# Turning eleven instead of ten key tiles on VectorE, with the query projection one slot earlier, in the attention stage of a decoder layer

## The reference

```python
C_q = Q @ Wq_d                                   # 128 latent columns
C_kv = K @ Wkv_d                                 # 64 latent columns for each of 1601 keys
CqWqk = (C_q @ W_qk).reshape(b, n, 16, 64)       # one 64-column query for each head
scores = einsum('bnhl,bkl->bhnk', CqWqk, C_kv) / 8
attn = softmax(scores, axis=-1)
V_up = (C_kv @ Wv_u).reshape(b, nkv, 16, 64)
out = einsum('bhnk,bkhd->bnhd', attn, V_up)      # x = layernorm(x + out)
```

## Time and profile before

| | |
|---|---|
| median of three runs | 2862.83 us (2859.35 to 2862.97) |
| the profiled execution | 2854.49 us, span 2852.5 us |
| granted TensorE clock, mean | 0.977 |
| busy in the span: TensorE, VectorE, GpSimd, ScalarE | 92%, 79%, 68%, 59% |
| exchange, DMA issues | 1152 of 80 KB |

### The profile page before, as it was taken

How to read it: one execution, slowest core, us unless ns; L and a number is a source line. 1 busy time by engine, 2 the same in 40 slices (tenths; PEclk the granted TensorE clock), 3 DMA queues, 4 the chain that set the end, 5 groups by cost and what they waited for, 6 DMA issues and landing times. The chain is left out here.

```text
span 2852.5 us, 41197 instructions
## 1 busy us (share of the span) xinstructions
PE 2636.4 (92%) x14360; PEld 1988.6 (70%) x14360; DVE 2264.6 (79%) x2125; ACT 1671.3 (59%) x2611; POOL 1941.2 (68%) x1423
## 2 busy tenths in 40 slices
PE   6867889999999999999996999999999999999997
PEld 3645566666666666666664788888888888788885
DVE  1436568888887788878884799999999899899988
ACT  2242467777777777777775545444545555555553
POOL 1000247767777777767874888888887788888883
PEclk9979999999999999999998999999999999999999
DMA  7304566767777777677765132222222322232221
GB/s 263 120 31 171 170 227 201 222 194 207 216 216 213 226 215 220 199 235 243 226 200 186 55 108 96 74 74 74 74 67 91 109 75 89 74 116 77 74 96 74
DMA packets 166768, 420.60 MB, mean 147 GB/s; under 512 B 30113, under 2 KB 57634, under 8 KB 166050
## 3 DMA queue, kind: packets, MB, share of 16 engines
q1 hardware_dynamic: 161698, 407.93, 45.7%
q10 hardware_dynamic: 4864, 10.03, 0.9%
HBM read 248.43 MB, written 75.04 MB: 113 GB/s over the span
## 5 line engine op out<-in xcount | busy, mean ns | idle before, releaser
L1566 DVE SCALAR_TENSOR_TENSOR c_acc<-c_ps,c_sd,c_acc 128x1024 f32<-128x1024 f32 x448 | 573.2, 1282 | 97.0 <-PE c_ps L1422 96.9
L1160 POOL COPY b_pt<-b_tn 32x640 f32<-32x640 f32 x640 | 457.6, 715 | 262.6 <-DVE b_tn L1068 231.0
L1477 ACT ACTIVATE c_scaled<-c_ps,c_sgu 128x1024 f32<-128x1024 f32 x336 | 375.6, 1118 | 425.0 <-PE c_ps L1422 422.5
L1062 DVE TENSOR_REDUCE b_nm<-b_sc 128x1 f32<-128x1604 f32 x256 | 468.1, 1828 | 189.4 <-PE b_sc L899 188.2
L981 ACT ACTIVATE b_pr<-b_sc,b_nm 128x799 f32<-128x799 f32 (+1 forms) x512 | 476.9, 934 | 237.3 <-DVE b_nm L1062 214.7
L1649 POOL TENSOR_TENSOR c_sum_u<-c_sum_u,c_scaled 128x1024 f32<-128x1024 f32 x168 | 404.9, 2410 | 116.0 <-ACT c_scaled L1477 115.5
L1649 POOL TENSOR_TENSOR c_sum_g<-c_sum_g,c_scaled 128x1024 f32<-128x1024 f32 x168 | 405.0, 2411 | 82.5 <-ACT c_scaled L1477 82.4
L899 PE MATMUL b_sc<-b_kh,b_qs 128*128 128x402 f32 (+1 forms) x1024 | 403.3, 394 | 41.2 <-ACT b_pr L981 37.5
L918 PE MATMUL b_po<-b_pt,shared 128*64 128x256 f32 x2560 | 389.4, 392 | 29.5 <-DMA b_pt<-b_tn 29.1
L1068 DVE STREAM_TRANSPOSE b_tn<-b_pr 128x1280 f32<-128x1280 f32 x256 | 384.7, 1503 | 3.3 <-ACT b_pr L981 2.0
L899 PE MATMUL b_sc<-b_kl,b_qs 128*128 128x402 f32 (+1 forms) x1024 | 357.3, 349 | 0.0
(11 more groups left out here) (192 smaller groups left out, 4371.6 us busy)
## 6 DMA issues: line engine op xcount, KB each, us to landing
b_pt<-b_tn SPq DMA_DIRECT2D x1152, 80.0 KB, 2.7
c_uw_int<-wint_u SPq DMA_DIRECT2D x56, 512.0 KB, 3.4
c_gw_int<-wint_g SPq DMA_DIRECT2D x56, 512.0 KB, 3.4
c_dw_int<-wint_d SPq DMA_DIRECT2D x56, 512.0 KB, 3.4
a_cx<-in_b_ctxT SPq DMA_DIRECT2D x16, 1608.0 KB, 11.1
b_rw<-in_c_gw SPq DMA_DIRECT2D x28, 512.0 KB, 4.1
b_rz<-in_c_gz SPq DMA_DIRECT2D x28, 512.0 KB, 5.6
b_rw<-in_c_uw SPq DMA_DIRECT2D x28, 512.0 KB, 4.0
```

Source lines behind the costliest of these rows:

```text
L1062: V.tensor_reduce(nm[:, u % 2:u % 2 + 1], both, AXY, ALU.max, negate=True).then_inc(s_nm, 1)
L1160: G.tensor_copy(pt[s][32 * c:32 * c + 32, a, :, :], tn[s][32 * a:32 * a + 32, c, :, :]).then_inc(s_block, 1)
L1477: S.activation(dst[:, :], pair[SLOT[x, t] % 4][:, :], ACT.Identity, scale=scale(x, t)).then_inc(s_e, 1)
L1566: V.scalar_tensor_tensor(out=total, in0=pair[SLOT[x, t] % 4][:, :], scalar=scale(x, t), in1=total, op0=ALU.mult, op1=ALU.add).then_inc(s_a ...
```

## The change

NDT goes from 10 to 11, so VectorE turns 1408 columns instead of 1280, each block move has 704 columns instead of 640 (88 KB instead of 80 KB in each DMA), TensorE transposes two tiles instead of three, and the copy to `pe` has 256 columns instead of 384. `project` moves from k % 8 == 5 to k % 8 == 4 on all engines. The value product is cut into tiles 0 to 7 and 8 to 12. The key buffers `kh` and `kl` shrink from 1664 to 1608 columns, which makes room for the larger `tn` and `pt`.

```diff
-NDT = 10
+NDT = 11
...
+KSC = 1608
...
 def ring_events():
     out = [("project", 0, 0)]
     for k in range(NU + OUT_AT):
-        if k % 8 == 5 and k + 3 < NU:
-            out.append(("project", (k + 3) // 4, 0))
+        if k % 8 == 4 and k + 4 < NU:
+            out.append(("project", (k + 4) // 4, 0))
...
 def special(k):
-    return k in CN_AT or k % 8 == 5 and k + 3 < NU or k % 4 == OUT_AT % 4 and k >= OUT_AT
+    return k in CN_AT or k % 8 == 4 and k + 4 < NU or k % 4 == OUT_AT % 4 and k >= OUT_AT
...
-        kh = [sb(f"b_kh{j}", [P, KPAD], F32R) for j in range(2)]
-        kl = [sb(f"b_kl{j}", [P, KPAD], F32R) for j in range(2)]
+        kh = [sb(f"b_kh{j}", [P, KSC], F32R) for j in range(2)]
+        kl = [sb(f"b_kl{j}", [P, KSC], F32R) for j in range(2)]
...
-                for t in (range(0, 7), range(7, NKT))[part]:
+                for t in (range(0, 8), range(8, NKT))[part]:
...
             for k in range(NU + OUT_AT):
                 if k < NU:
                     scores(k, 1)
-                if k % 8 == 5 and k + 3 < NU:
-                    project((k + 3) // 4)
+                if k % 8 == 4 and k + 4 < NU:
+                    project((k + 4) // 4)
...
             for t in (kh[0], kl[0], kh[1], kl[1]):
-                ins = V.memset(t[:, NKV:KPAD].bitcast(F32), 0.0)
+                ins = V.memset(t[:, NKV:KSC].bitcast(F32), 0.0)
```

## The result

The changed kernel takes 2882.91 us (median of six runs, 2876.13 to 2888.77) against 2863.21 for the kernel before: a ratio of 1.0069, 95% interval [1.0054, 1.0084], 19.7 us slower. The profiled execution has a span of 2878.8 us.

The account below looks back on a forecast made before the run. The prediction saw no engine full and took attention to be bound by a ring of waits, 4.06 us per plain slot. Octet +1, statistics +4, `cn` +1 and exchange +22 sum to +28: 2890 us, range 2862 to 2912.

Parts of the forecast that it names:

- the octet: Eight successive undisturbed slots of the attention order: 33.92 us against 33.9 before, +1 us in all.
- the exchange: Attention's transfers of turned blocks: late landings hold the value product for 46 us against 24, +22 us.
- The project slot: Attention slot holding `project`, now k=4: casts queue behind `cross`, next maximum at 5.50 us where it was 4.86.
- The output slots: Attention slots k=2 and k=6, where `output` is added, bound by TensorE: 4.28 and 4.45 us both become 4.06.
- two weight loads less, so -0.22: Even-slot value product on TensorE, five tiles instead of six; 12 loads take 1.43 us, so 0.22 us less.
- The odd slots: Plain odd attention slots: one tile more, one turn less, +0.12 us on TensorE, covered by 0.30 slack, 0.18 left.
- Statistics and `cn`: Layer norm statistics in slots 20 and 28, 0.65 us each, +4 us; six `cn` slots 0.12 each, +1 us.
- lost 2 us of budget: Pair 1's time from second transpose's end to the value product three slots on: was 10.0 us, now 8.04.
- the first rival: Transfer landings move with the load, pair 1 takes 7.1 us, late total stays 24: +6, 2869 us; chance 0.14.
- some 75 as its sign: Sign of being right: the value product's waits for the exchange rise from 45 to some 75 us.
- the fast one: Rival: casts in the project slot are not held up, slot 4.99 us, octet 33.4, total 2847 us; chance 0.11.
- the exchange becomes the bound: Rival: each late exchange delays the store and loads behind it, late total 75 us, +57, 2919 us; chance 0.12.

Follow-up runs that it names:

- e2_move_alone: The kernel before with only `project` moved to k % 8 == 4: 2878.04 us, ratio 1.0059.
- e3_cross_behind: The changed kernel with ScalarE's two `cross` copies of slots k % 8 == 3 run after the second half's exponent in the project slot: 2871.45 us, ratio 1.0039.
- e4_split_alone: The kernel before with only the value product cut 8/5 instead of 7/6: 2864.84 us, ratio 1.0006.
- e8_third_copy: The kernel of e1_project_back with one of nine block transfers made a third ScalarE copy at the odd slot's start: 2849.95 us, ratio 0.9959.
- the two light kernels: The changed kernel and the kernel before, each with the zero-point load cut to 128 of 1024 columns: 2865.16 us and 2851.29 us.
- e7_output_last: The kernel of e1_project_back with GpSimd's addition of the head's output behind the weight block's subtraction and cast: 2861.08 us, ratio 1.0000.
- e1_project_back: The changed kernel with `project` back in slots k % 8 == 5, eleven turned tiles and 8/5 split kept: 2864.17 us, ratio 1.0005.

## Why the prediction was right, and where its terms were off

The forecast was +28 us, measured +19.7; the direction and both places were right. That the sum came this near is in part luck: the octet cost 5 us more than forecast, while the exchange and the statistics cost less, and a term that the sum lacked gave some back.

- **The project slot**: forecast 5.50, measured 5.45, from the copies of `cross` (1.58 for 1.61) and the casts at 1.72 (1.75). e2_move_alone shows it without the rest of the change (5.31), e3_cross_behind removes it by ScalarE's order alone (4.97). The mechanism is shown.
- **The output slots**: forecast 4.06 both, measured 4.17 both. The step that failed is "two weight loads less, so -0.22": e4_split_alone shows that ten loads take the time of twelve, since five tiles take the three steps of six. The prediction divided 1.43 us by the 12 loads of the earlier trace rows, as if each had a time of its own; they are 12 of 14 (the first two lie ahead of that row), and they go in couples of tiles. The turn that went gave 0.11 (forecast 0.09), and k=6 lost the 0.17 as argued (4.28 in e2_move_alone). So the octet grew by 0.20 and not by 0.05: +6 us for the +1 of the sum.
- **The odd slots**: forecast 0.18 us of slack left, measured 0.41. The eighth tile cost nothing, as it joins the seventh, which ran alone; only the turn counted. Weight loads of slot 71 of the changed kernel, where the earlier trace rows had 0.30:

```profile
705.58 1.49 PEld L919 LDWEIGHTS b_po<-b_pt,shared 128*64 128x64 f32 x16 [0.27 <-issue]
707.46 0.20 PEld L929 LDWEIGHTS b_mi<-ident,b_pr 128*128 128x128 f32 x2 [0.39 <-issue]
...
708.70 0.19 PEld L900 LDWEIGHTS b_sc<-b_kh,b_qs 128*128 128x128 f32 x1 [0.41 <-ACT b_pr L982]
```

- **Statistics and `cn`**: forecast 0.65 each in six slots, +4 us. Slot 212, behind an undisturbed slot, took 6.02 against 5.45; slot 84 took 5.57, and slots 28 and 36, which also follow a `cn` slot, 5.00: 0.57 both times. The mechanism is right; but five of the six slots stand behind a lengthened one and are shorter for it (next point), so together they took only 1.7 us over 5.45. The `cn` slots, forecast +1, took 5.0 where they had taken 5.1 and 5.3: -0.9. In slot 84 VectorE goes from the transpose through the statistic into the maximum without idle:

```profile
765.21 1.65 DVE L1069 STREAM_TRANSPOSE b_tn<-b_pr 128x1408 f32<-128x1408 f32 x1
766.78 0.65 DVE L1085 BATCH_NORM_STATS2 b_stats<-b_y 128x6 f32<-128x512 f32 x1
767.46 1.83 DVE L1063 TENSOR_REDUCE b_nm<-b_sc 128x1 f32<-128x1604 f32 x1
```

- **A term that the sum lacked**: when slot k=3 is lengthened (a late exchange, a `cn` slot), ScalarE's copies are done earlier against the next maximum, and the project slot behind takes 5.0 to 5.3. That gave 4.0 us back in the slots without a statistic.
- **The exchange**: forecast +22, measured +16.7 by two traces, and less if the low value before is allowed for. The size was mis-set by carrying each pair's old landing time over. Pair 1 (p mod 4), which lost 2 us of budget, landed sooner after its transpose, 8.28 us on average instead of 8.97, as the first rival said: its slot k=7 rose by 5 us only. Pair 3, whose transpose follows the one before by 7.6 us, landed 0.28 later and slot k=3 rose by 8; pair 0 rose by 3, where I expected fewer. SyncE's queue waited 56.9 us for GpSimd's cast in the changed kernel and 35.8 before. That the nine transfers and the traffic beside them set much of the waits is shown by e8_third_copy and the two light kernels; that GpSimd's chain adds to pair 3's is argued only, and e7_output_last, with 12 us less of waiting for the cast and no fewer waits behind it, does not support it. TensorE's loads waited 64.5 us for the exchange, where the prediction had named some 75 as its sign.
- **The larger effect I had not separated**: more waits come with eleven tiles even where `project` stays (e1_project_back): 15 us over the trace before, 8 over e4_split_alone. That every budget of the exchange shrinks when the octet does is my explanation; the longer transfers and copies are another, and no run parts them. Nor do the parts add up: against the trace before, eleven tiles bring 15 us of waits, the move 16, both together 17. The move's 17 us over before (e2_move_alone) and 19 over e1_project_back agree.

Of the rivals, the fast one (casts not held up) is refuted by the slot itself, and "the exchange becomes the bound" never came to 75 us of waits. The prediction put a TensorE transpose at 0.09 us against the 275 ns that the Trainium skill gives ("TensorE: Matmul & The Clock Gate", Part 4, for bf16). The trace bears out both, for different things: a float32 transpose has a duration of 273 ns (median of the turns before), but they overlap, and the turn that went shortened the output slots by 0.11. For one turn less in a run the prediction's choice was right. The turns of the kernel before (ns, min/median/max):

```profile
L928 PE MATMUL b_mi<-ident,b_pr x768: 270/273/477, 397.1 to 1518.1; 128*128 128x128 f32 x192
```

The constant 2.0 us of the Trainium skill's "DMA: Bandwidth & Descriptors" (Anatomy of one DMA, given for the GpSimd path) is seen as the shortest landing in every kernel, though these transfers are SyncE's; its formula has no term for other traffic, and here the median landing fell from 2.7 to 2.1 in the kernel before with a narrower load beside it.

## What to carry to other kernels

A step that moves by one slot must be costed in each engine's own queue, behind what stands at the end of the slot before: here 1.6 us of copies ahead of two casts made a slot 0.6 us longer and undid what shorter slots gave. Where a chain of transfers takes 7 to 10 us and has a budget of 8 to 10, every slot made shorter takes from its cover; relieve the chain first (one transfer of nine less was worth 14 us with eleven tiles and some 10 with ten), and then shorten the slots. And where the tiles of a product run in couples, count couples: the eighth tile was free here, and five tiles took as long as six.

## What was not expected of the hardware

TensorE's time for the value product did not follow the number of its weight loads: in even slots 10 and 12 loads both took 1.44 to 1.45 us to the next instruction, in odd slots 14 (683.71 - 681.84 = 1.87, before) and 16 (698.82 - 696.94 = 1.88, changed) as well. What it follows is the number of couples of tiles, three and four, where a tile alone counts as one: a matmul of an even and one of an odd tile, which write different halves of `po`, start within 0.01 us of each other, and the next two 0.216 us later. From the first to the last start of a product it is 1.13 us with 10 matmuls and 1.14 with 12, 1.56 with 14 and 1.57 with 16 (medians).

Each of these products ends in 0.38 or 0.39 us without a weight load, which the profile puts down to "issue". TensorE isn't idle then: by the row of the kernel before, its last two matmuls start at 696.94 and run 0.39 us, past the next load at 697.26.
